# A routed expert FFN at the end of a graph network kernel: row numbers, second bias and weight transfers handled another way

## The reference, cut to what matters

```python
leaf = jnp.zeros((N,), jnp.int32)
for d in range(depth):                       # depth 4, E_ = 16
    logits = xf @ Wr[off:off + cnt].T + br[off:off + cnt]
    sel = jnp.take_along_axis(logits, leaf[:, None], axis=1)[:, 0]
    leaf = leaf * 2 + (sel > 0).astype(jnp.int32)
onehot = jax.nn.one_hot(leaf, E_, dtype=xf.dtype)
def body(acc, params):
    w1, bb1, w2, bb2, m = params             # (512, 2048), 2048, (2048, 512), 512
    h = jax.nn.gelu(xf @ w1 + bb1, approximate=False)
    y = h @ w2 + bb2
    return (acc + m[:, None] * y, None)
```

## Time before, and how to read the profile

| | us |
|---|---|
| Median of 3 runs (612.63 to 615.91) | 613.92 |
| Profiled execution, device time | 611.82 |
| Its span, from first to last instruction | 609.9 |
| Start of tile 0's first layer in it | 301.42 |
| End of the last tile's second layer in it | 602.1 |
| PE busy in the span | 532.0 (87%) |
| Transfers on SP's queue, share of 16 engines' span | 57.9% |

### The profile page before, as it was taken

How to read it: one execution, slowest core, us unless ns; L and a number is a source line. 1 busy time by engine, 2 the same in 40 slices (tenths; PEclk the granted TensorE clock), 3 DMA queues, 4 the chain that set the end, 5 groups by cost and what they waited for, 6 DMA issues and landing times.

```text
span 609.9 us, 9957 instructions
## 1 busy us (share of the span) xinstructions
PE 532.0 (87%) x3090; PEld 284.6 (47%) x3090; DVE 191.5 (31%) x600; ACT 160.8 (26%) x548; POOL 62.4 (10%) x88
## 2 busy tenths in 40 slices
PE   1967878889899999999895999999998778878994
PEld 1534555544356657444451555555543344334463
DVE  5997777482520010146740101111111001100100
ACT  1667778202011101002120222222222022202311
POOL 3000000021000000000012221221112120212021
PEclk9979999999999999999897999999999999999998
DMA  6169900100202010024686979999999999999980
GB/s 122 13 223 429 429 21 5 30 0 0 87 1 70 0 36 33 0 89 140 226 352 253 420 304 423 421 426 421 424 425 420 422 428 425 421 422 432 418 338 7
DMA packets 25209, 145.71 MB, mean 239 GB/s; under 512 B 10335, under 2 KB 12585, under 8 KB 16738
## 3 DMA queue, kind: packets, MB, share of 16 engines
q1 hardware_dynamic: 21986, 142.91, 57.9%
q0 software_dynamic: 3200, 2.50, 2.0%
HBM read 142.38 MB, written 4.72 MB: 241 GB/s over the span
## 4 chain that ended last, share of the span: by engine, by line
PE 58%; DMA 20%; DVE 8%; ACT 6%; issue 5%; ACTq 2%; POOL 0%; DVEq 0%; SPq 0%; POOLq 0%
DMA w<-in_L_ffn_W 18%; PE P L952 13%; PE P L1000 11%; PE P L839 8%; PE P L849 7%; PE P L858 4%; ACT H L537 2%; PE P L693 2%; ACT H L543 2%; PE P L969 2%; DVE stats L1134 2%; DMA XT<-normed_rows,C 1%; PE P L986 1%; PE P L802 1%; PE P L801 1%
## 5 line engine op out<-in xcount | busy, mean ns | idle before, releaser
L952 PE MATMUL P<-w,H 128*64 128x512 f32 x480 | 108.6, 600 | 17.1 <-DMA w<-in_L_ffn_W 15.8
L1000 PE MATMUL P<-w,FB 128*64 128x256 f32 x1024 | 115.6, 381 | 5.5 <-DMA w<-in_L_ffn_W 5.5
L629 ACT ACTIVATE FB<-P,FB 128x64 f32<-128x64 f32 x256 | 54.3, 362 | 156.2 <-PE P L969 156.2
L1000 PEld LDWEIGHTS P<-w,FB 128*64 128x64 f32 x1024 | 72.0, 137 | 43.9 <-issue 10.7
L1392 DVE COPY H<-P 128x512 f32<-128x512 f32 x32 | 22.1, 692 | 215.2 <-PE P L952 215.2
L693 PE MATMUL P<-H 125*125 125x500 bf16 x176 | 59.6, 414 | 18.5 <-ACT H L543 18.0
L952 PEld LDWEIGHTS P<-w,H 128*64 128x64 f32 x480 | 35.9, 138 | 81.6 <-issue 60.5
L1116 DVE TENSOR_SCALAR H<-iota,small 125x626 bf16<-125x626 f16 x176 | 60.2, 382 | 14.0 <-issue 8.9
L839 PE MATMUL P<-G,XT 128*125 128x512 f32 x120 | 52.0, 592 | 0.0
L693 PEld LDWEIGHTS P<-H 125*125 125x125 bf16 x176 | 25.1, 143 | 44.5 <-ACT H L543 30.9
L849 PE MATMUL P<-C,H 125*128 125x313 f32 (+1 forms) x160 | 42.4, 425 | 0.0
(11 more groups left out here) (294 smaller groups left out, 441.9 us busy)
## 6 DMA issues: line engine op xcount, KB each, us to landing
w<-in_L_ffn_W SPq DMA_DIRECT2D x62, 2048.0 KB, 28.7
G<-in_L_gnn_W SPq DMA_DIRECT2D x3, 1024.0 KB, 5.3
xs<-in_x SPq DMA_DIRECT2D x1, 1120.0 KB
out<-xs SPq DMA_DIRECT2D x5, 224.0 KB
normed_rows<-xn SPq DMA_DIRECT2D x5, 224.0 KB
G<-in_L_ffn_W SPq DMA_DIRECT2D x1, 1024.0 KB, 5.0
C<-in_L_ffn_W SPq DMA_DIRECT2D x1, 1024.0 KB, 5.3
xs<-in_L_ffn_W SPq DMA_DIRECT2D x1, 1024.0 KB, 7.3
```

The lines of the kernel that those rows point to most:

```text
L629: g = nc.scalar.activation(hT[:, m, :], P[:, 3 + rd, c * SA:(c + 1) * SA], ACT.Gelu, bias=bT[b][:, m:m + 1])
L952: mm = nc.tensor.matmul(P[g * SA:(g + 1) * SA, h, :], xT[b][:, k, :], w1a[k][:, h, g], start=(k == 0), stop=(k == KD - 1))
L1000: mm = nc.tensor.matmul(P[g * SA:(g + 1) * SA, 7, 0:256], hT[:, m, :], w2_sb[b][:, m, g * 256:(g + 1) * 256], start=False, stop=(m == MH - 1))
```

## The change

1. **Tile 1's row numbers by themselves.** DVE makes the selector of tile 1 (`slots`) from expert 1's ranks, as it does tile 0's; PE multiplies it with the node numbers (10 matmuls with one column) right behind `turn_rows(0)`; DVE turns the result into row numbers (`row_one`). POOL gathers tile 1's rows by them, without waiting for `number_rows`. PE turns these rows ahead of the fourth quarter of tile 0's second layer, before it was behind it.
2. **b2 by DMA.** The two matmuls for b2 in each tile, and the b2 rows in `FB`, are gone. DVE makes each node's expert number (`expert_of`), POOL gathers each node's row of b2 (5 transfers of 125 rows of 2 KB), and then adds these to `out` (5 accumulating transfers of the same size). The loop of gathers and scatters begins when these additions have landed (`s_b2st`).
3. **The largest expert is tile 10** (`LARGE`) instead of tile 14. All loops are split around it. Its additional second-layer matmuls stand between quarters.
4. **W1 and W2 in four transfers of 1 MB each** (54 halves after the table become 108 quarters, and the 8 early halves become 16). The first layer goes block by block: for k, for both halves h; each block is given back as soon as it is used. Before, blocks (0, 1) for both halves, then (2, 3).

```diff
-            pool.wait_ge(s_gh, NCH * 3)
-            nc.gpsimd.memset(b2_rows, 0.0).then_inc(s_b2z, 1)
-            pool.sem_inc(s_yfree, 2)
...
+            pool.sem_inc(s_yfree, 1)
...
+            pool.wait_ge(s_ost, 16 * 2 * NCH)
+            pool.wait_ge(s_eid, 1)
+            for c in range(NCH):
+                nc.gpsimd.indirect_dma_start(out=b2_tok[c][0:NC, :], out_offset=None, in_=b2,
+                                             in_offset=bass.IndirectOffsetOnAxis(ap=expert_of[0:NC, c:c + 1], axis=0),
+                                             bounds_check=NE - 1, oob_is_err=False).then_inc(s_b2, 16)
+            pool.wait_ge(s_xst, 16 * 2 * NCH)
             pool.wait_ge(s_xT, 1)
-            gather(1, 1)
-            pick(row_inB, 2, 2 * last, 2)
+            pool.wait_ge(s_idx1, 1)
+            nc.gpsimd.indirect_dma_start(out=x_row, out_offset=None, in_=x_dram.rearrange("t (g n) -> (t g) n", g=2),
+                                         in_offset=bass.IndirectOffsetOnAxis(ap=row_one, axis=0),
+                                         bounds_check=2 * N_NODES - 1, oob_is_err=False).then_inc(s_xr, 16)
+            pool.wait_ge(s_b2, 16 * NCH)
+            for c in range(NCH):
+                nc.gpsimd.indirect_dma_start(out=out, out_offset=bass.IndirectOffsetOnAxis(ap=row_of[0:NC, c:c + 1], axis=0),
+                                             in_=b2_tok[c][0:NC, :], in_offset=None,
+                                             bounds_check=N_NODES - 1, oob_is_err=False, compute_op=ALU.add).then_inc(s_b2st, 16)
...
+            pick(row_outB, 1, LARGE, 2)
+            pool.wait_ge(s_b2st, 16 * NCH)
+            pool.sem_inc(s_yfree, 1)
```

```diff
             def load_w1(i, b, user):
...
-                for j in range(2):
-                    if j == 0:
-                        sp.wait_ge(s_w1u, user + 1)
-                    else:
-                        sp.wait_ge(s_h, 2 * user + 2)
-                    sp.dma_start(w1_sb[b][:, 2 * j:2 * j + 2, :],
...
+                for k in range(KD):
+                    j, r = k // 2, k % 2
+                    sp.wait_ge(s_w1u, KD * user + k + 1)
+                    sp.dma_start(w1_sb[b][:, k:k + 1, :],
...
-                for h in range(2):
-                    sp.wait_ge(s_l2, 4 * (i - 2) + 2 * h + 2)
...
+                for q in range(4):
+                    h, r = q // 2, q % 2
+                    sp.wait_ge(s_l2, 4 * (i - 2) + q + 1)
```

```diff
+            tt(slots[0:NC], iota[0:NC, 0:SA].unsqueeze(1).to_broadcast([NC, NCH, SA]),
+               rank01[0:NC, :, 1:2].to_broadcast([NC, NCH, SA]), ALU.is_equal).then_inc(s_selx, 1)
+            link(tt(val[0:NC], leaf[0:NC], iota[0:NC, 0:NE].unsqueeze(1).to_broadcast([NC, NCH, NE]), ALU.mult))
+            link(nc.vector.tensor_reduce(not01.rearrange("p c t -> p (c t)")[0:NC, 0:NCH], val[0:NC], AX.X, ALU.add))
+            ts(row_of[0:NC, :], token[0:NC, :], -1.0, None, ALU.add)
+            nc.vector.tensor_copy(expert_of[0:NC, :], not01.rearrange("p c t -> p (c t)")[0:NC, 0:NCH]).then_inc(s_eid, 1)
...
             copy_inputs(0, 0)
+            dve.wait_ge(s_row1, 1)
+            v = P[:, 5, 384:385]
+            link(ts(row_one_f, v, 0.5, EMPTY, ALU.is_lt, ALU.mult))
+            link(stt(row_one_f, v, 2.0, row_one_f, ALU.mult, ALU.add))
+            tt(row_one, row_one_f, half_of, ALU.add).then_inc(s_idx1, 1)
```

More of the change, by code:

```diff
@@ L63 @@
 FIXED = 3
+LARGE = 10
 MORE = (N_NODES - 1) // SA
@@ L649, in _ @@
             for b in range(2):
-                tile_out(last, b, end=True)
+                tile_out(LARGE // 2, b)
+            with act.Fori(LARGE // 2 + 1, last) as p:
+                for b in range(2):
+                    tile_out(p, b)
+            for b in range(2):
+                tile_out(last, b)
         @block.tensor
@@ L933, in tile @@
                 i = 2 * p + b
-                more = end and b == 0
+                more = isinstance(p, int) and i == LARGE
                 first = isinstance(p, int) and i == 0
@@ L982, in tile @@
                 turn(3, 0).then_inc(s_hT, 1)
-                pe.wait_ge(s_bTc, i + 1)
-                pe.wait_ge(s_ycp, i + 1)
-                for g in range(2):
-                    nc.tensor.matmul(P[g * SA:(g + 1) * SA, 7, 0:256], bT[b][:, MH:MH + 1].to_broadcast([128, SA]),
-                                     b2_rows[:, g * 256:(g + 1) * 256], start=True, stop=False)
-                if not (first or end and b):
+                if not (first or end):
                     pe.wait_ge(s_xr, 16 * i + 16)
@@ L1022, in tile @@
                         slot_tokens()
+                    if first and q == 3:
+                        pe.wait_ge(s_xr, 16)
+                        turn_rows(1)
                     second_a(q)
-                if first:
-                    pe.wait_ge(s_xr, 16)
-                    turn_rows(1)
-                if more:
-                    for q in range(4):
-                        mm = second_b(q)
-                    mm.then_inc(s_l2B, 1)
             for p in range(2):
@@ L1036, in _ @@
             last = pe.value_load(npairs_t[0:1, 0:1], min_val=NE // 2 - 1, max_val=MAX_PAIRS - 1)
-            with pe.Fori(2, last) as p:
+            with pe.Fori(2, LARGE // 2) as p:
                 for b in range(2):
@@ L1047, in _ @@
             for b in range(2):
-                tile(last, b, end=True)
+                tile(LARGE // 2, b)
+            with pe.Fori(LARGE // 2 + 1, last) as p:
+                for b in range(2):
+                    tile(p, b)
+            for b in range(2):
+                tile(last, b, end=(b == 1))
         @block.vector
@@ L1399, in tile_copies @@
                     number_rows()
-                if not (end and b):
+                if not end:
                     copy_inputs(i + 1, 1 - b)
@@ L1404, in _ @@
                 tile_copies(0, b)
-            with dve.Fori(1, last) as p:
+            with dve.Fori(1, LARGE // 2) as p:
                 for b in range(2):
@@ L1411, in _ @@
             for b in range(2):
-                tile_copies(last, b, end=True)
+                tile_copies(LARGE // 2, b)
+            with dve.Fori(LARGE // 2 + 1, last) as p:
+                for b in range(2):
+                    tile_copies(p, b)
+            for b in range(2):
+                tile_copies(last, b, end=(b == 1))
 _INS = ["x", "src", "dst", "L0_gnn_W_conv", "L0_gnn_b_conv", "L0_gnn_W_lin", "L0_gnn_b_lin", "L0_ffn_Wa", "L0_ffn_ba",
```

204 lines of the change are left out of this document (107 added, 97 removed).

## The result

| | before | after |
|---|---|---|
| Median, us | 614.22 (4 runs) | 631.45 (4 runs, 630.46 to 633.74) |
| Profiled execution / its span, us | 611.82 / 609.9 | 631.85 / 630.1 |
| Last second layer ends, us | 602.1 | 621.3 |
| Bytes of SP's queue from 308 to 380 us, MB | 25.23 | 17.43 |

The account below looks back on a forecast made before the run. Bound by the weight stream's start after the table, its bytes and gaps, and PE's work behind the last byte. Terms -4.3 + 1.3 - 7.7 + 5.1 = -5.6 us took the median from 613.92 to 608.3 us; range 604.6 to 616.

Parts of the forecast that it names:

- Start of the stream: First weight issue after the table: additional DVE steps delay tile 0 and the table, +1.3 us.
- Tile 1: Tile 1's rows are there by 308 us, its 7.1 us stall goes, it starts at 321.2; gaps closed, -7.7 us.
- b2's gathers: Five gathers of b2 rows from 298 us: costed at nothing, 2 us if they ran into the stream.
- The new wait: Tile 2's rows, behind the additions' landing, at 330 to 334; PE waits 1 to 5 us: 0, up to +1.
- rival 1: b2's 125-row transfers load engines unevenly, some with 50 rows instead of 39: 609.7 to 614.8 us, chance 0.22.
- Rival 2: The additions land too late, tile 2's rows come at 340, PE waits 11 us: +1.4 us, 615.3; chance 0.14.
- its dearer case: Late additions with uneven rows as well, 42 contending rows, tile 2's rows at 347: +8.9 us, 622.8.
- 4.8 us to spare: Slack before the weight stream runs dry: busy until 354.3 us, tile 2's first second-layer quarter at 348.3.
- b2's traffic: Additions of 625 rows of 2 KB inside the weight stream, 0.13 us a row: +5.1 us, from 3.5 to 7.0.
- Quarters: 54 more weight transfers, 1 MB each, cost at most 1.8 us; taken as 0 from loads at 431 GB/s.
- The end, -4.3: Largest expert as tile 10 and weights in quarters: last second layer ends at 597.8 instead of 602.1 us.

## Why the prediction was wrong, point by point

**Start of the stream, +1.3.** Right: the first issue came at 307.84 against 306.24, +1.6; tile 0 started at 302.60 as said. A kernel profiled twice began 1.4 us apart, so the tenths are luck. Behind it nothing was lost to the gathers, as the kernel without additions shows.

**Tile 1.** Right: it started at 322.51 (said: 321.2, the first layer of tile 0 ran at a lower clock and took 8.8 us). The stall is gone, and its part alone is worth 7.7 us (0.9874 of 613.9), with an interval of 5.4 to 10.1; that it is 7.7 to the tenth is luck.

**b2's gathers, 0.** Right in the stream, wrong for GpSimd. They landed 5.7 to 8.3 us after their issue, the last at 312.6, and so the additions began 8 us later than in my sum. In the changed kernel this turned out to cost little, since a start 2.4 us earlier (in halves) landed no earlier.

**The new wait, 0: packets per row.** This is the step that failed. I wrote "about a packet per row" and meant the turns behind weights: 0.31 + 0.13 us for each of 32 contending rows of an engine, landed at 324 to 328. The turn itself was nearly right, one packet of SP's for one of POOL's. But an addition of 125 rows was 416 packets, not 144, so an engine had 130 turns and not 45; the landing came at 351, tile 2's rows at 355.2, and PE waited 25.06 us, not 1 to 5. I had the earlier trace rows with 144 packets for the scatter of 128 rows, and no row of before shows what 125 rows would be. My rival 1 had the cause (five engines instead of 16) and drew the wrong thing from it, 50 rows on some engines instead of 39. What it does is to give all 16 engines 130 turns. Rival 2 had the consequence, the slow clock and a stall moved by one tile; its dearer case, both together, gave +8.9 us for rows at 347. They came at 355.2.

**The new wait: when the rows start.** The packet count is not all of it. With 144 packets (the run with 128 rows) the rows still came at 344.1, PE waited 12.82 us, and the kernel had lost 15 us to the additions, 7.0 of them traffic. I had the additions start at 305.7, 8 rows of each engine through before the stream, and 14 us for the rest. There they were issued from 310.11, the first packets showed from 314.5 on, in a full stream, and all 45 turns contended: 45 x (0.31 + 0.18) are 22 us, which gives 336.5, and the last landing was at 336.7. So the term of 0 would have failed even with the packets that I had reckoned with, by some 8 us. Of its inputs, the scatter's delay of 7.1 us is 10.8 - 3.3 = 7.5 in the earlier trace rows, too little to matter.

**"4.8 us to spare."** The figures beside it give 354.3 - 348.3 = 6.0, and where the other 1.2 went isn't worked out. As a bound it held: with rows at 329.8 nothing was lost, with rows at 337.15 hardly anything (0.9 us of gaps). Beyond that nearly every us of delay was a us of stream: with the same packets, rows at 344.11 in place of 337.15 made the span 5.6 us longer for 7.0 us.

**b2's traffic, +5.1.** Mis-sized. A row took about 0.18 us of an engine (7.0 us x 16 for 625 rows), the upper end of my bound, not 0.13. In the changed kernel only about 4.9 of them fell into the stream, since the last rows went when it was dry.

**Quarters, 0.** Wrong by 4.5 us of rate. The 431 GB/s of three 1 MB loads were 3 us in a quiet spell, and a window of 80 us was needed. The end, -4.3, was right, and so parts 3 and 4 together are worth nothing that can be told: 0.9874 without them, 0.9858 with.

The sum as it came out, on the profiled executions: 7.8 MB fewer by 380 us are +18.4 us at 424 GB/s; the lower rate from 380 to 619 is +4.2; the end is -4.3. That is +18.3 of 19.2 us by which PE ended later.

## What to carry to other kernels

Before a transfer of GpSimd's goes into a full stream, count its packets and not only its bytes or rows: here each took a turn behind one packet of weights, and 128 partitions for 125 cut them to a third. A wait for such a landing is best read as a queue: whatever is issued behind it on the same queue waits too, with or without an instruction that says so. And work taken from PE is worth nothing where the DMA engines set the end; the version with b2 on PE, 604 to 605 us, beats both kernels.

## What the runs showed of the hardware

- Two queues with work shared the DMA engines packet by packet, tiny packets too: 949 to 947 with 8 KB on the other side, 506 to 481 with 16 KB, each in 20 us; in the latter kernel two windows of 2 us went otherwise (205 to 60, 248 to 51). The Trainium skill ("DMA: Bandwidth & Descriptors", Queues, rings and completion order) has engines take turns between queue rows by packets of typically some 9 to 17 descriptors. Both rows agree with the turns; whether a packet of the profile is such a packet no row shows.
- An accumulating transfer of 125 rows of 2 KB was 416 packets and a gather of 125 rows 224, by the counts of the pages; with 128 partitions the two together were 224, which fits 144 and 80.
- An addition's packets showed in the DMA engines some 5 us after its issue began: issued at 310.11, 312.27 and 313.57, first packets at 314.5 to 315, 317 to 317.5 and 318.5 to 319.
- Weights in transfers of 1 MB ran at 417 GB/s against 424 with 2 MB, each over 80 us with full engines (share 1.02 and 1.01).
- Alone, rows of 2 KB that are added to DRAM passed at 57 a us, 117 GB/s at a share of 0.63, in the run in halves from 347 to 349 us; that is 0.18 us of an engine each. Weights there ran at 422 GB/s from 400 to 560.

What stays open: which engines the tiny packets went to, why q0 twice passed more than one for one, what gaps the first part alone leaves in a typical execution, and whether additions spread over later tiles, in the slack of GpSimd's queue, would cost only their 7 us. That wasn't tried; if they cost these 7 us, it would end behind the version with b2 on PE.
